# Order of maxima and values in a self-attention, PSUM banks of its last steps, and zeroing of the keys on VectorE

## The chip, the cores and the metric

The kernel runs on one core of a Trainium2 chip. The metric is the device time in microseconds of one execution, and a kernel's figure is the median of its runs. A profile is one execution of its own, taken by the hardware profiler.

## What is computed

Four stages are applied to x (4 samples, 1024 tokens, 256 channels), all in float32. L0 is a routed mixture of three small networks and a gate. L1 and L2 are transformer blocks, each with self-attention, cross-attention over 77 context tokens and a feed-forward part; L3 is one more cross-attention. The self-attentions matter here; this is the one of L1, cut:

```python
def mha(x, ctx, wq, bq, wk, bk, wv, bv, wo, bo, mask=None):   # 16 heads of 16 channels
    q = (x @ wq + bq).reshape(Bq, Nq, H, HD)
    k = (ctx @ wk + bk).reshape(Bq, Nk, H, HD)
    v = (ctx @ wv + bv).reshape(Bq, Nk, H, HD)
    scores = jnp.einsum('bqhd,bkhd->bhqk', q, k) / np.sqrt(HD)
    attn = jax.nn.softmax(scores, axis=-1)
    return jnp.einsum('bhqk,bkhd->bqhd', attn, v).reshape(Bq, Nq, D) @ wo + bo
h = layernorm(x, ln1_g, ln1_b)
h = mha(h, h, sa_wq, sa_bq, sa_wk, sa_bk, sa_wv, sa_bv, sa_wo, sa_bo)
x = x + h + t_sa[:, None, :]
```

L2 has the same with a modulated layernorm and with `x = x + g_sa * x_sa`.

## The kernel before

**The order of work.** One loop over the four samples does L0. A second one ("blocks") does L1, L2 and L3 for one sample per pass. Its work is a list of named steps, PASS, written by `pass_schedule`: L1sa, L1ca, L1mlp, L2sa, L2ca, L2mlp, L3ca. Every engine walks through the same list and issues its own part of each step; semaphore counts are taken from the position of a step in the list. So the list is the order on each of the in-order engines. SP's DMAs have a list of their own (`stack_maxima`, the DMA is L591).

**The steps of a self-attention.** Almost all matmuls go through a helper at L634, so its line stands for most of TensorE's rows.

- N, T: a half of the tokens is normalised (DVE L1417) and transposed (TensorE L919, copied by ACT L1149).
- P, K: a projection of q or k (c = half of the channels, n = half of the tokens), split into a high and a low part by ACT and POOL; then selection matmuls that place pairs of heads into qs or ks, one head in each 64-row stack. K carries a pattern of four letters, one for each tile: "a" and "d" say that ACT or DVE evicts it, "-" that it isn't done in this step; small letters are matmuls over 32 rows, capital letters matmuls over all 128 rows.
- V: the values of two token tiles (8 matmuls), evicted by ACT (L1325). V0 to V3 make up all eight tiles.
- A(g, n, t, j): scores of one token tile against all keys, only for their maxima: two matmuls into two neighbouring banks and a DVE tensor_reduce over 1024 elements into mxh (L1683). A group (g, n), four heads and half of the tokens, has 16.
- both, M: DVE joins the maxima of a group into mx (L1692); TensorE transposes mx (L1036, four transposes), ACT copies the result to mrow (L1350), SP's DMA puts mrow into row 32 of the qs stacks. The pair is called the group's turn. With that row the scores come out with the maximum taken off.
- S(g, n, kt, j): transposed scores of one key tile (kt, 8 of them) and one head; ACT's exp writes probs (L1366). PV multiplies probs by v into bank 7.
- O, OT: behind the last key tile of a group ACT copies bank 7 to ow (L1372), TensorE transposes ow (L1082), DVE divides by the sums (L1708, L1710) into tok.
- aT, o: tok is transposed (L1091, ACT L1377) and multiplied by the output weights; DVE adds to x (L1649; in L2 after the gate, L1644). scond, R and add put bias rows onto x (ACT L1299, TensorE, DVE L1601, POOL L1787).

A self-attention is 8 groups of 8 units, unit u being (g, n, kt). The order in a unit is: S for two heads, OT if one is due, PV of the unit two before, S for two more heads, and then as many maxima as `more` allows. The maxima run ahead of the scores: before unit 0 stands the front with 19 of them, the first 16 each with a projection, stack or values step beside it. Units 0 to 4 then take 2, 3, 3, 3, 3 maxima, the later ones 2 each, and the last falls in unit 52. The turn of a group stands inside the maxima of the next: "both" follows two of them and M follows three (for the very first turn, "both" follows none and M one).

**Banks.** In a self-attention TensorE's steps other than PV take banks from banks 0 to 6 by least recent use (`shared`); A takes two neighbours. A step waits until the engine that read the bank before is done. The other modules have small rings of their own: 0 and 1 (with 6 and 7 for maxima) and 2 to 5.

**The cross-attention behind a self-attention** begins inside its tail (`cross_lead`). Its keys are placed in kz, which POOL has to zero first ("zero", L1803). In `cross_attention` the stack of q ("AAAA", ACT L1334) stands ahead of the transpose of the second token half, T(1).

## Time and profile before

| | us |
|---|---|
| median of 3 runs | 4191.32 (4186.39 to 4198.61) |
| profiled execution | 4198.08 |
| its span, first to last instruction | 4196.3 |
| TensorE busy | 3678.6 (88%) |
| ACT busy | 2353.3 (56%) |
| DVE busy | 2214.9 (53%) |
| granted TensorE clock, mean | 0.933 |

Busy shares are averages over stages with different limits. The granted clock is a share of full speed: 1.00 is 2.4 GHz, 0.50 is 1.2 GHz. In a row of the timeline, `[0.51 <-DVE mxh L1683]` says that the engine sat idle for 0.51 us and that the DVE instruction of line 1683, writing mxh, ended this. PE is TensorE, PEld its loading of weights. x2 behind an operation is two instructions in a row, and the time is that of both together. In the table by stretch, x behind a busy time is the number of instructions.

### The profile page before, as it was taken

To read this page: it belongs to the slowest core of one execution; us is meant where nothing else is said; L and a number is where in the kernel's file an instruction comes from. 1 tells how busy PE (TensorE), PEld (TensorE's weight loads), DVE (VectorE), ACT (ScalarE), POOL (GpSimd) and SP (SyncE) were. 2 spreads that over 40 slices of the span, in tenths; PEclk is the share of its full clock that TensorE was granted. 3 is DMA by queue.
4 is the path that set the end of the run, shared out by engine and by line. 5 is a ranking of instruction groups with operands and counts; after the bars stand their busy time and mean duration, and the time that the engine had idled before them with its cause. 6 is when DMAs were issued, how large, how long until landed. Compare 5 with 4: busy or idle time off the path is not lost.

```text
span 4196.3 us, 65738 instructions
## 1 busy us (share of the span) xinstructions
PE 3678.6 (88%) x20057; PEld 2127.3 (51%) x20057; DVE 2214.9 (53%) x3552; ACT 2353.3 (56%) x4082; POOL 864.1 (21%) x558
## 2 busy tenths in 40 slices
PE   7999988889888878889888788898889788898888
PEld 5777674346434743356336543464347333563356
DVE  4332435743674447644755457436744566437644
ACT  2333335764676456764666457646764567546754
POOL 3222221014102410033005110241023100240041
PEclk8999998999999989999999989999999899999999
DMA  3000110001000010000000100010000100000010
GB/s 125 31 1 31 31 37 34 2 27 41 1 1 12 31 42 1 16 32 21 1 1 33 50 1 1 27 41 1 1 12 31 42 1 17 31 21 1 1 31 22
DMA packets 70782, 92.76 MB, mean 22 GB/s; under 512 B 9227, under 2 KB 57934, under 8 KB 70350
## 3 DMA queue, kind: packets, MB, share of 16 engines
q1 hardware_dynamic: 40958, 63.40, 4.5%
q10 hardware_dynamic: 29520, 25.39, 1.9%
q8 instruction: 181, 2.97, 0.3%
q14 instruction: 123, 1.01, 0.1%
HBM read 77.96 MB, written 9.50 MB: 21 GB/s over the span
## 4 chain that ended last, share of the span: by engine, by line
issue 79%; POOL 16%; PE 3%; DVE 0%; POOLq 0%; ACT 0%; DMA 0%; SPq 0%; ACTq 0%; DVEq 0%
POOL hidl L1761 3%; PE ps L634 3%; POOL hidl L1796 3%; POOL x L1787 2%; POOL ql L1820 2%; POOL small L1721 1%; POOL kl L1820 1%; POOL hTl L1728 1%; POOL W2h L1811 1%; POOL W1h L1811 1%; POOL W1l L1813 0%; POOL W2l L1813 0%; POOL kz L1803 0%; DMA sel_in<-in_sel 0%; DVE tok L1417 0%
## 5 line engine op out<-in xcount | busy, mean ns | idle before, releaser
L1683 DVE TENSOR_REDUCE mxh<-ps 128x2 f32<-128x1024 f32 x1024 | 1211.1, 1220 | 419.9 <-PE ps L634 416.2
L1366 ACT ACTIVATE probs<-ps 128x512 f32<-128x512 f32 (+1 forms) x2176 | 1215.0, 629 | 380.2 <-PE ps L634 374.5
L634 PE MATMUL ps<-probs,v 128*32 128x512 f32 (+1 forms) x4864 | 680.0, 632 | 3.8 <-ACT probs L1366 3.8
L634 PE MATMUL ps<-qs,ks 64*128 64x512 f32 x2048 | 559.4, 486 | 11.0 <-DVE mxh L1683 9.7
L634 PEld LDWEIGHTS ps<-qs,ks 64*128 64x128 f32 x2048 | 261.4, 190 | 539.6 <-ACT probs L1366 355.1
L1721 POOL TENSOR_TENSOR small<-small 128x4 f32<-128x4 f32 x66 | 68.3, 1035 | 2246.6 <-DVE small L1411 2246.6
L634 PE MATMUL ps<-ks,qs 64*128 64x512 f32 x2048 | 413.0, 462 | 128.2 <-DVE mxh L1683 100.3
L634 PEld LDWEIGHTS ps<-ks,qs 64*128 64x128 f32 x2048 | 202.7, 191 | 331.5 <-DVE mxh L1683 226.8
L634 PE MATMUL ps<-hT,slot 128*128 128x512 f32 x448 | 247.7, 687 | 24.2 <-ACT hT L1149 9.2
L634 PE MATMUL ps<-slot,hT 128*128 128x256 f32 x896 | 238.6, 415 | 14.8 <-ACT hT L1377 9.3
L1680 DVE TENSOR_REDUCE mx<-ps 128x4 f32<-128x312 f32 x384 | 167.4, 478 | 117.6 <-PE ps L634 113.9
L1334 ACT ACTIVATE qs<-ps,cols 128x512 fp32r<-128x512 f32 x288 | 178.6, 692 | 73.7 <-PE ps L634 73.7
L634 PEld LDWEIGHTS ps<-slot,hT 128*128 128x128 f32 x896 | 177.7, 207 | 75.3 <-issue 21.7
L1761 POOL TENSOR_TENSOR hidl<-hid,hidh 128x512 fp32r<-128x512 f32 x96 | 127.6, 1333 | 334.6 <-ACT hid L1233 334.6
L634 PEld LDWEIGHTS ps<-probs,v 128*32 128x32 f32 (+1 forms) x4864 | 97.0, 109 | 157.9 <-issue 78.2
L1820 POOL TENSOR_TENSOR ql<-whole,qh 128x512 fp32r<-128x512 f32 x80 | 102.0, 1275 | 316.1 <-ACT whole L1319 316.1
L1796 POOL TENSOR_TENSOR hidl<-hid,hidh 128x512 fp32r<-128x512 f32 x128 | 161.9, 1291 | 10.9 <-ACT hid L1384 9.0
L1649 DVE TENSOR_TENSOR x<-x,ps 128x512 f32<-128x512 f32 x80 | 55.0, 687 | 189.9 <-PE ps L634 189.9
L1230 ACT ACTIVATE hidh<-ps,cols 128x512 fp32r<-128x512 f32 x96 | 66.3, 690 | 158.2 <-PE ps L634 158.1
L1708 DVE RECIPROCAL rc<-ps 128x16 f32<-128x16 f32 x160 | 40.6, 254 | 203.0 <-PE ps L1082 203.0
L634 PE MATMUL ps<-kz,qs 128*128 128x156 f32 x768 | 131.2, 296 | 17.9 <-ACT hT L1149 5.7
L634 PE MATMUL ps<-W2h,hidh 128*128 128x256 f32 x512 | 145.2, 284 | 0.0
(220 smaller groups left out, 6134.1 us busy)
## 6 DMA issues: line engine op xcount, KB each, us to landing
slot<-in_L_w SPq DMA_DIRECT2D x8, 1024.0 KB, 7.7
slot<-in_L_fc_w SPq DMA_DIRECT2D x8, 1024.0 KB, 5.2
adw<-in_L_adaln_w SPq DMA_DIRECT2D x4, 1536.0 KB, 6.5
xin<-in_x ACTq DMA_DIRECT2D x5, 1024.0 KB, 5.6
x_after_block<-x ACTq DMA_DIRECT2D x20, 256.0 KB, 2.3
xin<-x_after_block ACTq DMA_DIRECT2D x5, 1024.0 KB, 5.5
ew<-in_L_e_w SPq DMA_DIRECT2D x6, 768.0 KB, 12.3
x<-in_x ACTq DMA_DIRECT2D x4, 1024.0 KB, 7.3
```

The costliest lines, as they stand in the source:

```text
L634: return pe.matmul(out, lhsT, rhs, start=start, stop=stop)
L1230: act.activation(hidh0[:, (E * n + e) % 2, m % 4, :], src, ACT.Silu, bias=col("L0_e_b1", m))
L1334: ins = act.activation(qs[:, pair, n * HALF:(n + 1) * HALF], ps[:, b, :], ACT.Identity, bias=qs_rows)
L1366: ins = act.activation(dst, src, ACT.Exp, scale=SCALE)
L1680: dve.tensor_reduce(mx[:, z, t, j0:j0 + GH], ps[:, a, 0:GH * SP_].rearrange("p (j s) -> p j s", s=SP_), AX.X, ALU.max, negate=True).then_i ...
L1683: dve.tensor_reduce(mxh[:, z, t, j // 2, j % 2, :], ps[:, a:a + 2, :], AX.X, ALU.max, negate=True).then_inc(dve_done, M.add(dve_done, name))
L1721: pool.tensor_tensor(rstd[:, tt], ve[:, tt], nhalf[:, tt], ALU.pow).then_inc(pool_done, M.add(pool_done, (tag, "rstd", h)))
L1761: pool.tensor_tensor(hidl0[:, (E * n + e) % 2, m % 4, :], hid0[:, m % 4, :], hidh0[:, (E * n + e) % 2, m % 4, :].bitcast(F32), ALU.subtrac ...
L1787: pool.tensor_tensor(x[:], xin[:] if tag == "L1sa" else x[:], rrow[:].unsqueeze(1).to_broadcast([P, NT, D]), ALU.add).then_inc(pool_done, ...
L1796: pool.tensor_tensor(hidl[:, n, m, :], hid[:, n, m, :], hidh[:, n, m, :].bitcast(F32), ALU.subtract).then_inc(pool_done, M.add(pool_done, ...
L1811: pool.tensor_tensor(hi[:], w, zero.unsqueeze(2).to_broadcast(w.shape), ALU.add).then_inc(pool_done, M.add(pool_done, name + ("hi",)))
L1820: pool.tensor_tensor(lo[:, c, part], whole[:, whole_of(name)[0], 0:kn], hi[:, c, part].bitcast(F32), ALU.subtract).then_inc(pool_done, M.a ...
```

## The change

- Turns: "both" comes directly behind the last maximum of its group, and M four maxima of the next group later (one later for the very first turn).
- Values: V1 and V2 leave the front, V3 leaves unit 1, and they stand in units 0, 1 and 2, between the first two scores and PV.
- Front: the stacks of q(1,0), q(1,1) and k(1,1) are done in capitals, over 128 rows (k(1,1) was already); the four half stacks of q have an empty place after each; both half stacks of k(1,1) move from unit 0 to ahead of it. The front holds 20 maxima instead of 19, units 0 to 3 take 3 each and the others 2, and the last is in unit 51.
- End of a self-attention: aT(0), o0, o1 and the next N0 come one unit earlier. OT(3,1), aT(1,0), aT(1,1), o2 and o3 use the banks 6, 7, 6, 7, 6 and are no longer in the shared order.
- Cross-attention behind a self-attention: "zero" is a DVE memset behind T(0) and OT(3,1) instead of a POOL addition ahead of T(0); T(1) and eight maxima come before the q stack "AAAA", which had stood behind four.

```diff
@@ -148,17 +148,16 @@
             for n in range(NH):
                 scores = [("A", g, n, t, j) for t in range(TPH) for j in range(GH)]
 
-                first = 0 if (g, n) <= (0, 1) else 2
-                maxima += scores[:first] + turn[:1] + scores[first:first + 1] + turn[1:] + scores[first + 1:]
+                behind = 1 if (g, n) == (0, 1) else 4
+                maxima += turn[:1] + scores[:behind] + turn[1:] + scores[behind:]
                 turn = [("both", g, n), ("M", g, n)]
         maxima += turn
 
-        def halves(which, c, n):
-            return [("K", "aa--", which, c, n), ("K", "--aa", which, c, n)]
-
-        beside = ([("P", "k", 1, 0)] + halves("q", 0, 1) + [("P", "q", 1, 1)] + halves("k", 1, 0) + [("P", "k", 1, 1)] + halves("q", 1, 0)
-                  + [("V", 1)] + halves("q", 1, 1))
-        later = [("K", "AA--", "k", 1, 1), ("K", "--AA", "k", 1, 1), ("V", 3)]
+        def halves(which, c, n, who="a"):
+            return [("K", 2 * who + "--", which, c, n), ("K", "--" + 2 * who, which, c, n)]
+
+        beside = ([("P", "k", 1, 0)] + halves("q", 0, 1) + [("P", "q", 1, 1)] + halves("k", 1, 0) + [("P", "k", 1, 1)]
+                  + [w for k in halves("q", 1, 0, "A") + halves("q", 1, 1, "A") for w in (k, None)] + halves("k", 1, 1, "A"))
         taken = 0
 
         def more(upto):
@@ -171,13 +170,10 @@
         first_slot = GH * TPH
         for i in range(first_slot):
             more(i + 1)
-            put(tag, *beside[i:i + 1])
-        assert len(beside) <= first_slot
+            put(tag, *[w for w in beside[i:i + 1] if w])
         more(first_slot + 1)
-        put(tag, *[("scond",)] * (tag == "L1sa"), ("R",), ("add",))
-        more(first_slot + 2)
-        put(tag, ("V", 2))
-        lead = first_slot + 3
+        put(tag, *beside[first_slot:], *[("scond",)] * (tag == "L1sa"), ("R",), ("add",))
+        lead = first_slot + 4
         more(lead)
         lag = 2
         units = [(g, n, kt) for g in range(GROUPS) for n in range(NH) for kt in range(NT)]
@@ -186,6 +182,8 @@
         for u in range(end + lag):
             if u < end:
                 put(tag, *[("S",) + units[u] + (j,) for j in range(2)])
+            if u < 3:
+                put(tag, ("V", u + 1))
             if turn is not None:
                 put(tag, ("OT",) + turn)
                 turn = None
@@ -197,23 +195,22 @@
                     turn = unit[:2]
             if u < end:
                 put(tag, *[("S",) + units[u] + (j,) for j in range(2, GH)])
-                put(tag, *(later[:2] if u == 0 else later[2:] if u == 1 else []))
-                more(lead + min(3 * u, 2 * u + 4) + 2)
-
-            if u == end - 5:
+                more(lead + min(3 * (u + 1), 2 * (u + 1) + 4))
+
+            if u == end - 6:
                 put(tag, *[("aT", 0, c) for c in range(KC)])
-            elif u in (end - 4, end - 3):
-                put(tag, ("o", u - end + 4))
-            elif u == end - 2:
+            elif u in (end - 5, end - 4):
+                put(tag, ("o", u - end + 5))
+            elif u == end - 3:
                 put(follow, ("N", 0))
 
     def cross_lead(tag, before):
 
         first, then = projections("q", 0)
         if before:
-            put(tag, ("zero",), ("T", 0))
+            put(tag, ("T", 0))
             put(before, ("OT", GROUPS - 1, NH - 1))
-            put(tag, *projections("k", 0))
+            put(tag, ("zero",), *projections("k", 0))
             put(before, *[("aT", NH - 1, c) for c in range(KC)])
             put(tag, ("K", "dddd", "k", 0, 0), first)
             put(before, ("o", 2))
@@ -229,11 +226,10 @@
         def singles(which, c, n):
             return [("K", "-" * i + "A" + "-" * (PAIRS // KC - 1 - i), which, c, n) for i in range(PAIRS // KC)]
 
-        put(tag, *maxima[:4], ("K", "AAAA", "q", 1, 0))
         if before:
-            put(tag, ("T", 1), *maxima[4:8], ("P", "q", 0, 1), *maxima[8:10], ("V", 0), ("P", "q", 1, 1))
+            put(tag, *maxima[:4], ("T", 1), *maxima[4:8], ("K", "AAAA", "q", 1, 0), ("P", "q", 0, 1), *maxima[8:10], ("V", 0), ("P", "q", 1, 1))
         else:
-            put(tag, *maxima[4:6], ("P", "q", 1, 1), *maxima[6:10], ("V", 0))
+            put(tag, *maxima[:4], ("K", "AAAA", "q", 1, 0), *maxima[4:6], ("P", "q", 1, 1), *maxima[6:10], ("V", 0))
         put(tag, *maxima[10:14], ("K", "aaaa", "q", 0, 1), *maxima[14:16])
         put(tag, ("add",), ("M", 0, 0))
         for i, k in enumerate(singles("q", 1, 1)):
@@ -860,6 +856,7 @@
                 "L2mlp": [("L2mlp_g", silu_of(adw[:, :, 5 * D:6 * D]) + [pick("g_ff")]), ("L2mlp", [pick("fc2_b")])],
                 "L3ca": [("L3ca", [pick("bp")])],
             }
+            TAIL = {("OT", (GROUPS - 1, NH - 1)): 0, ("aT", (NH - 1, 0)): 1, ("aT", (NH - 1, 1)): 0, ("o", (2,)): 1, ("o", (3,)): 0}
             rings = {"small": 0, "single": 0, "wide": 0}
             used = [0] * 7
             M.open("blocks")
@@ -887,6 +884,9 @@
                         return tuple(range(b, b + count))
 
                     def small():
+                        if not alone and (kind, step[1:]) in TAIL:
+                            b = 6 + TAIL[kind, step[1:]] % 2
+                            return b, (b,)
                         if not alone:
                             banks = shared(2 if kind == "A" else 1)
                             return banks[0], banks
@@ -1334,7 +1334,7 @@
                                 ins = act.activation(qs[:, pair, n * HALF:(n + 1) * HALF], ps[:, b, :], ACT.Identity, bias=qs_rows)
                             elif cross:
                                 if tag != "L3ca":
-                                    act.wait_ge(pool_done, upto(pool_done, (tag, "zero")))
+                                    act.wait_ge(dve_done, upto(dve_done, (tag, "zero")))
                                 for e in range(2):
                                     r = stacked(e, 0, STACK)
                                     ins = act.activation(kz[r, pair, e, :], ps[r, b, 0:SP_], ACT.Identity, bias=ks_rows[r])
@@ -1604,6 +1604,9 @@
                             dve.wait_ge(conditions_loaded, upto(conditions_loaded, "all"))
                             dve.tensor_scalar(mrowb[:], mi[:], 0.0, MASKED, ALU.is_equal, ALU.mult).then_inc(dve_done, M.add(dve_done, "mrowb"))
                             dve.tensor_scalar(mcolb[:], mic[:], 0.0, MASKED, ALU.is_equal, ALU.mult).then_inc(dve_done, M.add(dve_done, "mcolb"))
+                    elif kind == "zero":
+
+                        dve.memset(kz[:].bitcast(F32), 0.0).then_inc(dve_done, M.add(dve_done, name))
                     elif kind == "mod" and tag == "L2sa":
                         dve.wait_ge(mm_done, upto(mm_done, name))
                         b = M.where(name)
@@ -1662,7 +1665,7 @@
                             b = M.where((tag,) + stack)
                             if cross:
                                 if tag != "L3ca":
-                                    dve.wait_ge(pool_done, upto(pool_done, (tag, "zero")))
+                                    dve.wait_ge(dve_done, upto(dve_done, (tag, "zero")))
                                 for e in range(2):
                                     r = stacked(e, 0, STACK)
                                     ins = dve.tensor_scalar(kz[r, pair, e, :], ps[r, b, 0:SP_], ks_rows[r], None, ALU.add)
@@ -1795,12 +1798,6 @@
                         pool.wait_ge(act_done, upto(act_done, name))
                         pool.tensor_tensor(hidl[:, n, m, :], hid[:, n, m, :], hidh[:, n, m, :].bitcast(F32), ALU.subtract
                                            ).then_inc(pool_done, M.add(pool_done, name))
-                    elif kind == "zero":
-
-                        before = MODULES[[m for m, _ in MODULES].index(tag) - 1][0]
-                        pool.wait_ge(mm_done, upto(mm_done, (before, "S", GROUPS - 1, NH - 1, NT - 1, GH - 1)))
-                        flat = kz[:].rearrange("p c e s -> p (c e s)")
-                        pool.tensor_tensor(flat, zero.to_broadcast(flat.shape), zero.to_broadcast(flat.shape), ALU.add).then_inc(pool_done, M.add(pool_done, name))
                     elif kind == "split":
 
                         w, hi, lo, loaded = (W1, W1h, W1l, slot_loaded[2]) if step[1] == "W1" else (W2, W2h, W2l, slot_loaded[3])
```

## Rows read from the trace of the kernel before

**Rows 1.** The page: busy time of each engine, share, instructions.

```profile
PE 3678.6 (88%) x20057; PEld 2127.3 (51%) x20057; DVE 2214.9 (53%) x3552; ACT 2353.3 (56%) x4082; POOL 864.1 (21%) x558
```

**Rows 2.** Timeline, steady unit: start, busy us, engine, line, operation.

```profile
739.85 0.73 PE L634 MATMUL ps<-ks,qs 64*128 64x512 f32 x4 [0.51 <-DVE mxh L1683]
...
740.39 2.36 DVE L1683 TENSOR_REDUCE mxh<-ps 128x2 f32<-128x1024 f32 x2 [0.59 <-PE ps L634]
```

**Rows 3.** Stretches: start:end, length, busy PE, PEld, DVE, ACT, POOL, clock, DMA.

```profile
654.50:692.60 38.10, 32.16 (x114) 15.88 (x115) 23.30 (x23) 17.74 (x29) 8.35 (x4) 0.82 0.00 1
692.60:726.10 33.50, 28.80 (x137) 12.74 (x136) 21.57 (x20) 20.60 (x39) 0.00 (x0) 0.90 0.00 1
726.10:854.70 128.60, 113.24 (x685) 46.79 (x688) 97.60 (x96) 90.93 (x172) 0.00 (x0) 0.96 0.01 2
...
752.40:777.20 24.80, 21.91 (x141) 9.09 (x144) 19.52 (x20) 18.15 (x36) 0.00 (x0) 1.00 0.00 1
...
1948.60:1983.40 34.80, 31.64 (x114) 15.69 (x115) 23.56 (x22) 16.25 (x27) 8.38 (x4) 0.85 0.00 1
1983.40:2015.90 32.50, 27.14 (x137) 11.58 (x136) 21.61 (x20) 20.60 (x39) 0.00 (x0) 0.95 0.00 1
2015.90:2142.50 126.60, 111.35 (x683) 46.58 (x682) 97.52 (x96) 90.56 (x172) 0.00 (x0) 0.97 0.01 1
```

**Rows 4.** Timeline, a turn of maxima and what follows.

```profile
744.71 0.68 PE L1036 MATMUL ps<-ident,mx 128*4 128x128 f32 x4 [1.17 <-DVE mx L1692]
...
745.50 0.59 ACT L1350 ACTIVATE mrow<-ps 4x512 f32<-4x512 f32 x1 [2.00 <-PE ps L1036]
...
748.95 2.36 DVE L1683 TENSOR_REDUCE mxh<-ps 128x2 f32<-128x1024 f32 x2 [3.16 <-PE ps L634]
```

**Rows 5.** Stretches of slow clock, in the front and at the turn.

```profile
676.80:690.50 13.70, 9.46 (x24) 5.50 (x22) 4.92 (x8) 2.07 (x3) 3.76 (x1) 0.50 0.00 1
745.10:748.50 3.40, 3.40 (x16) 0.99 (x15) 0.69 (x1) 1.67 (x3) 0.00 (x0) 0.50 0.01 2
```

**Rows 6.** Timeline, a unit with the transposes of ow.

```profile
758.21 0.66 PE L1082 MATMUL ps<-ident,ow 128*128 128x128 f32 x4
...
760.75 2.35 DVE L1683 TENSOR_REDUCE mxh<-ps 128x2 f32<-128x1024 f32 x2
```

**Rows 7.** Timeline behind an L2 self-attention: values, k selection.

```profile
1313.29 1.99 PE L634 MATMUL ps<-slot,hT 128*128 128x256 f32 x8 [1.36 <-ACT whole L1319]
...
1316.79 0.30 PE L634 MATMUL ps<-kh,sel 32*128 32x78 f32 x1 [1.27 <-DVE x L1649]
```

**Rows 8.** Timeline, front of the first L1 self-attention.

```profile
671.49 7.09 DVE L1683 TENSOR_REDUCE mxh<-ps 128x2 f32<-128x1024 f32 x6 [1.13 <-PE ps L634]
...
682.13 2.07 PE L634 MATMUL ps<-slot,scond 128*128 128x256 f32 x4 [2.27 <-ACT scond L1299]
...
686.85 3.77 PE L634 MATMUL ps<-slot,hT 128*128 128x256 f32 x8
```

**Rows 9.** Timeline, ACT in units without maxima.

```profile
874.03 8.03 ACT L1366 ACTIVATE probs<-ps 128x512 f32<-128x512 f32 x16 [1.47 <-PE ps L634]
```

**Rows 10.** Timeline, lead and first maxima of the L1 cross-attention.

```profile
906.48 0.90 PE L634 MATMUL ps<-kh,sel 32*128 32x78 f32 x4 [0.92 <-ACT hT L1377]
...
907.66 2.54 DVE L1668 TENSOR_SCALAR kz<-ps,cols 64x78 fp32r<-64x78 f32 x8 [3.90 <-PE ps L634]
...
924.88 2.42 ACT L1334 ACTIVATE qs<-ps,cols 128x512 fp32r<-128x512 f32 x4 [3.26 <-PE ps L634]
...
928.02 0.45 PE L634 MATMUL ps<-kz,qs 128*128 128x156 f32 x2 [1.21 <-ACT hT L1149]
```

**Rows 11.** One line: count, ns min/median/max, starts, form.

```profile
L1569 DVE MEMSET v<- x1: 3472/3472/3472, 625.4 to 625.4; 128x4096 f32 x1
```

**Rows 12.** Timeline, a cross-attention: mrow and what its DMA released.

```profile
949.70 0.57 ACT L1350 ACTIVATE mrow<-ps 16x512 f32<-16x512 f32 x1
...
953.37 0.46 PE L634 MATMUL ps<-qs,kz 64*77 64x512 f32 x2 [0.21 <-DMA qs<-mrow]
```

## The prediction

> **What bounds the kernel now.** The page comes first: TensorE is busy for 88% of the span and no other engine for more than 56% [rows 1], so the first guess is TensorE. The chain of waits on the page names nothing for most of the span, so the timeline of one steady unit of a self-attention comes next [rows 2]. There DVE reduces two maxima in 2.36 us and then waits 0.59 us for the matmuls of the next two, while TensorE itself had to wait 0.51 us for DVE before it could write them. The two form a loop through the PSUM banks: reduce, bank free, matmul, reduce. Its period is 2.36 + 0.59 = 2.95 us, 23.6 us for the 8 units of a group. What a self-attention costs beyond that is what the change can touch.
>
> The table by stage [rows 3] shows how much it is. Groups 1 to 5 of the first L1 self-attention take 128.6 us where 5 x 23.6 = 118.0 would do: 10.6 too long. Those of a later L2 one (second block) take 126.6: 8.6 too long. Group 0 takes 33.5 and 32.5 us. The front, from the first maximum to the first exponential, takes 38.1 and 34.8 us, with DVE busy for only 23.3 and 23.6 of them.
>
> Where the 10.6 us go is seen at a turn [rows 4]. TensorE arrives at the transposes of the maxima and waits 1.17 us for DVE's "both". The matmuls queued behind the transposes come late, and DVE's next reduce starts after 3.16 us of idleness where 0.59 is normal. Behind this turn there is a second loss: for 3.4 us the granted clock reads 0.50, that is 1.2 GHz [rows 5]; TensorE had stood still just before. One group in which the clock stays at 1.00 takes 24.8 us. If two of the five are like it, the other three take (128.6 - 49.6) / 3 = 26.3. So a turn costs 1.2 us by its wait (24.8 - 23.6) and a dip another 1.5.
>
> **Part 1: the turn.** "both" now stands straight behind the group's last maximum and the transposes four maxima further on. Two maxima are one unit, so "both" is by then at least one period old: the 1.17 us wait is gone, and with it what made DVE idle. The transposes remain, 0.68 us of TensorE [rows 4]; their cover is TensorE's own wait for DVE in each unit. The nearest row for work of this kind is the four transposes of ow, 0.66 us: the reduce behind them starts with no idleness at all [rows 6]. The ACT copy to mrow and the SP DMA move with the transposes; since more maxima are ahead, TensorE comes to them in the same unit as before, and nothing behind them on ACT or SP comes later. The upper end is all of the 10.6 (L1) and 8.6 us (L2). At the lower end the dips stay, three and two at 1.5 us: 6.1 and 5.6. I take 85% of the upper ends, 9.0 and 7.3, because the row of ow is the nearest; the rest is TensorE work that spills over. What is late next is the bank loop itself.
>
> **Part 2: group 0.** Its 8 units hold 20 maxima. From rows 2, a unit with three of them takes 3 x 1.18 + 0.59 = 4.1 us, so four such and four of 2.95 make 28.3 us. V1, V2, V3 (8 matmuls each, 1.99 us at full clock [rows 7]) now come in units 0, 1 and 2, between two scores and probs x v. Three maxima are six matmuls, some 1.1 us by the 0.73 us of four [rows 2], and four scores as much, so 1.99 us more fit into the 4.1 of units 0 and 1, which have no probs x v. In unit 2 probs x v adds about 1.1, and 1.0 is lost. ACT's copy of V, 0.6 us, stands beside four exponentials of 2.0 us [rows 9] and fits everywhere. The upper end is 33.5 - 29.3 = 4.2 for L1 and 3.2 for L2. At the lower end V runs at half clock (3.77 us [rows 8]) in all three units, which takes the gain and 3 us more: -3. I take 3.3 and 2.3, nearer to the upper end, since these units ran at 0.90 and 0.95 [rows 3].
>
> **Part 3: the front.** V1 leaves (DVE's wait behind it was 1.13 us), and V2, 3.77 us in which DVE soon stood idle [rows 8]: 4.9 us. Added are one more maximum and, behind the last slot, the second half stack of k11 with two ACT evictions: 0.8 us for its two matmuls at half clock (four take 0.73 at full clock, [rows 2]) and 2 x 0.6 for the evictions (four take 2.42, [rows 10]), 2.0 in sum. Net 2.9, the lower end. At the upper end the clock comes back in the 13.7 us at 0.50 [rows 5]: the four scond matmuls take 2.07 us there [rows 8] and the four rows matmuls are of the same shape, so 2.07 of both would return, and most of the 2.0 hides: 6.3 in L1; L2 has no scond, 4.9. The full-row selections (capitals) stream the same 512 columns; without a row of their own here I bound them by 0 and by 0.5 us for each of the four half stacks that are new in them, about half of what four 32-row selections take (0.90, [rows 10]), 2 us in sum, hidden by DVE's reduces in the slots where nothing now stands beside the maximum; I take nothing. I take 4.0 and 3.3 for the part, near the lower ends, because the first turn keeps only one maximum between "both" and its transposes, so the standstill before the slow stretch remains.
>
> **Part 4: the end of the maxima.** One more maximum ahead means that the last falls in unit 51. Four units without maxima take 8.03 us by ACT [rows 9], 2.0 each against 2.95: half of the difference, 0.5 us.
>
> **Part 5: tail, banks, cross lead.** OT(3,1), aT, o2 and o3 get banks 6 and 7 of their own; aT(0), o0, o1 and N0 start a unit earlier. In L1 the k selections wait 0.92 us for ACT, and the cross-attention's maxima wait 1.21 us for T(1)'s copy, which stood behind a whole q stack on ACT [rows 10]; T(0) comes perhaps 0.5 sooner, a quarter of a 2.0 us unit. Upper end 2.6, lower end 0; I take 1.5. In L2 TensorE waits 1.36 and 1.27 us at banks that ACT and DVE still read [rows 7]; with 1.2 and 0.5 as in L1 the upper end is 4.3, the lower 0; I take 3.2, as both waits are named.
>
> **Part 6: zero.** POOL's addition goes, DVE gets a memset of 1248 elements a row. The one memset in the trace does 4096 in 3.47 us [rows 11], so 1.06 us, at a place where DVE sits idle for 3.90 us before the k stack [rows 10]: nothing. Without that cover it would be 1.06 x 8 = 8.5 us in all.
>
> **The sum.** L1: 9.0 + 3.3 + 4.0 + 0.5 + 1.5 = 18.3. L2: 7.3 + 2.3 + 3.3 + 0.5 + 3.2 = 16.6. Each of the four blocks has one of both: 4 x 34.9 = 140 us. The profiled execution took 4198.1 us (1.8 more than its span), so it would take 4058; the median before is 4191.3, so 4051. All upper ends: 4 x (24.2 + 21.5) = 183, 4008. All lower ends: 4 x (6.5 + 6.0) = 50, 4141.
>
> **The rivals.** (a) The clock stays restless: 0.68 us of transposes in a full unit are followed by a stretch at half clock even without the wait. For it: the stretch of rows 5 begins within the transposes. Against: the transposes of ow are as long and fall into a group that runs at 1.00 [rows 3, 6]. Price: 5.5 dips per block at 1.5 us and 1 us at each front, 4 x 10 = 40: 4091. The Trainium skill's TensorE: Matmul & The Clock Gate, Part 4: PE-mode transpose, says that transposes do not count as busy time for the clock as matmuls do; by that rule this case would come. The group with the transposes of ow at 1.00 speaks against it at this size.
>
> (b) TensorE bounds group 0, V being paid at half clock. For it: the stretch just ahead reads 0.50 [rows 5]. Against: V has left that stretch. Price: part 2 at its lower end, 6.3 and 5.3 less, 46 in four blocks: 4097. The Trainium skill's TensorEngine Tiling (Array Packing), Key Properties, says that a change of tiling mode drains TensorE, and V between scores (64 rows) and probs x v (32 columns) adds one. By that rule each V would cost more than its 1.99 us. Nothing before shows V there; the full-size transposes between the same two cost DVE nothing [rows 6].
>
> (c) The wait only moves to the next bank, and parts 1 and 2 fall out. For it: DVE releases "both" and the banks alike. Against: the loop keeps 2.95 us in every unit but the turn's. What remains is 4 x (6.0 + 7.0) = 52: 4139.
>
> (d) It becomes slower. The first scores of a group need the row of maxima that SP's DMA puts into qs, two units (5.9 us) behind the transposes. The copy to mrow ends 1.4 us after these start [rows 4], which leaves 4.5; a landing takes 953.37 - 950.27 = 3.1 us [rows 12]; the margin is 1.4. If faster units and a busy queue eat it, TensorE stands at 7 group starts in each of 8 self-attentions, 56 in all. From 140 / 56 = 2.5 us per start the gain is gone; at 3.0 the time is 4191 - 140 + 168 = 4219. Against: a landing would have to take 7 us.
>
> **How the numbers follow.** The forecast, own range 4020 to 4075, has 0.55; more gain than that 0.04; (a) 0.17, (b) 0.12, (c) 0.06, (d) 0.03; and 0.03 that the parts lend each other's gain until nothing is measured. A measurement of this kernel tells a change from none at about 0.3%, 12.6 us. The range of 8 in 10 runs from 4015, below which only the sum of the upper ends lies, to 4105, which takes in (a) and (b). Faster: all but the last two, 0.94; same 0.03; slower 0.03.
>
> **What would show it.** Right: groups 1 to 5 near 24 us each; TensorE's transposes waiting for "both" only at the first and the last turn of a self-attention; no stretch at 0.50 behind a turn; a front of 34 us in L1 and a group 0 of 30. Wrong: transposes on time and DVE still idle for 3 us behind them (c); stretches at 0.50 elsewhere (a); V over 2 us in units 0 to 2 with DVE waiting (b); scores released by the DMA at group starts (d).

## The result, and the profile after

| | us |
|---|---|
| median of 4 runs | 4007.91 (4002.04 to 4025.84) |
| before, its 4 runs | 4194.23 (4186.39 to 4198.61) |
| ratio | 0.9565, 95% interval 0.9531 to 0.9599 |
| profiled execution, its span | 4009.09, 4007.3 |
| granted TensorE clock, mean | 0.956 (0.933 before) |

The change gives 186 us where 140 were forecast. 4008 us is below the range (4015 to 4105) and at the sum of all upper ends; the prediction gave 0.04 to more gain than its own range. The page of the changed kernel, against [rows 1]:

```profile
PE 3585.2 (89%) x20057; PEld 2109.6 (53%) x20057; DVE 2203.9 (55%) x3560; ACT 2353.9 (59%) x4082; POOL 845.4 (21%) x550
```

The instruction counts of TensorE and ACT are as before, yet TensorE is busy 93 us less: the same matmuls ran at a higher clock. The table by stretch, the answers to [rows 3], first L1 self-attention and the L2 one of the second block (front, group 0, groups 1 to 5):

```profile
654.00:685.40 31.40, 27.31 (x105) 13.28 (x103) 21.90 (x23) 19.39 (x30) 5.30 (x4) 0.96 0.01 1
685.40:718.00 32.60, 29.14 (x150) 14.56 (x149) 23.91 (x22) 19.52 (x37) 3.06 (x1) 0.93 0.01 1
718.00:836.10 118.10, 108.25 (x685) 45.89 (x688) 97.88 (x96) 90.55 (x170) 0.00 (x0) 1.00 0.01 2
1890.80:1918.70 27.90, 26.43 (x103) 12.81 (x103) 21.74 (x21) 17.90 (x28) 4.60 (x4) 1.00 0.00 1
1918.70:1949.40 30.70, 26.75 (x150) 13.31 (x149) 24.14 (x23) 19.50 (x36) 3.77 (x1) 1.00 0.00 1
1949.40:2067.40 118.00, 108.39 (x682) 46.01 (x680) 97.76 (x96) 90.43 (x171) 0.00 (x0) 1.00 0.01 2
```

Groups 1 to 5 take 118.1 and 118.0 us, which is 5 x 23.6, at a clock of 1.00. The fronts are 6.7 and 6.9 us shorter, with the clock at 0.96 and 1.00 (0.82 and 0.85 before). Group 0 is only 0.9 and 1.8 us shorter. A turn in the timeline, the answers to [rows 4]:

```profile
735.25 2.36 DVE L1686 TENSOR_REDUCE mxh<-ps 128x2 f32<-128x1024 f32 x2 [0.59 <-PE ps L630]
735.37 0.60 PE L1036 MATMUL ps<-ident,mx 128*4 128x128 f32 x4
...
738.20 2.36 DVE L1686 TENSOR_REDUCE mxh<-ps 128x2 f32<-128x1024 f32 x2 [0.60 <-PE ps L630]
```

TensorE does not wait before the transposes, and DVE is idle for 0.60 us behind them instead of 3.16. 738.20 - 735.25 is one period of 2.95 us: the transposes cost nothing.

Where the time came from, by the stages of all four blocks. Each boundary is the start of the first maximum, the start of unit 0's or a later unit's first exponential, the end of the last exponential, or the start of the cross-attention's first maximum. Means in us:

```
               front  g0    g1-5   g6,7+end  tail  rest to next self
L1 before      38.5   33.8  128.0  45.4      22.8  140.4
L1 after       32.8   32.3  118.1  46.0      19.1  139.1
L2 before      34.9   32.2  126.7  46.3      23.5  213.0
L2 after       27.9   31.2  118.2  45.8      17.6  210.3
gain, both     12.7    2.5   18.4  -0.1       9.6    4.0     = 47.1 per block, 188 in four
priced at       7.3    5.6   16.3   1.0       4.7 (both)     = 34.9 per block, 140
```

A second profile of the changed kernel has the same means within 1.4 us a stage; its tails and what follows them are in the last row of the table further below. Smaller differences between the mean lengths of two kernels are not read as effects, unless all four blocks show them alike.

### The profile page after: what moved, and what is told of

It is laid out like the page before. It is cut to its first block, busy times and chain, and to the rows that moved or that the text cites. A ratio compares the mean times of both kernels' runs of the same rounds, so it can differ in the third digit from the quotient of the medians.

```text
span 4007.3 us, 65762 instructions
## 1 busy us (share of the span) xinstructions
PE 3585.2 (89%) x20057; PEld 2109.6 (53%) x20057; DVE 2203.9 (55%) x3560; ACT 2353.9 (59%) x4082; POOL 845.4 (21%) x550
## 4 chain that ended last, share of the span: by engine, by line
issue 79%; POOL 16%; PE 3%; DVE 0%; POOLq 0%; ACT 0%; DMA 0%; SPq 0%; ACTq 0%; DVEq 0%
POOL hidl L1764 3%; POOL hidl L1799 3%; PE ps L630 3%; POOL x L1790 2%; POOL ql L1817 2%; POOL small L1724 1%; POOL kl L1817 1%; POOL hTl L1731 1%; POOL W2h L1808 1%; POOL W1h L1808 1%; POOL W1l L1810 0%; POOL W2l L1810 0%; DMA sel_in<-in_sel 0%; DVE tok L1417 0%; PE ps L1082 0%
## 5 line engine op out<-in xcount | busy, mean ns | idle before, releaser
L630 PE MATMUL ps<-probs,v 128*32 128x512 f32 (+1 forms) x4864 | 655.0, 611 | 6.3 <-ACT probs L1366 6.3
L630 PE MATMUL ps<-qs,ks 64*128 64x512 f32 x2048 | 538.3, 474 | 5.6 <-DVE mxh L1686 5.4
L630 PE MATMUL ps<-hT,slot 128*128 128x512 f32 x448 | 234.3, 654 | 27.9 <-ACT hT L1149 12.2
L630 PE MATMUL ps<-slot,hT 128*128 128x256 f32 x896 | 225.0, 398 | 9.3 <-ACT hT L1377 9.3
L630 PEld LDWEIGHTS ps<-slot,hT 128*128 128x128 f32 x896 | 168.5, 196 | 60.6 <-issue 21.6
L630 PE MATMUL ps<-W2h,hidl 128*128 128x256 f32 x512 | 147.1, 287 | 0.0
```

The source lines that it names most:

```text
L630: return pe.matmul(out, lhsT, rhs, start=start, stop=stop)
```

## The experiments

All ratios are of a kernel's runs to those of the kernel before on the same chip. For the whole change two such series exist, 0.9565 and, on another chip, 0.9551 (0.9513 to 0.9588). Single runs of one kernel differ by up to 37 us, longer ones having a lower mean clock, and L0, which no edit touches, ends between 646 and 661 us in the profiles. A gain taken from the ratio and the same gain taken from the medians can differ by 10 us. So below about 0.003 nothing is read from a ratio, and the stage lengths carry the argument.

**The turn alone**, on the kernel before:

```diff
-                first = 0 if (g, n) <= (0, 1) else 2
-                maxima += scores[:first] + turn[:1] + scores[first:first + 1] + turn[1:] + scores[first + 1:]
+                behind = 1 if (g, n) == (0, 1) else 4
+                maxima += turn[:1] + scores[:behind] + turn[1:] + scores[behind:]
```

> The kernel before with nothing changed but the place of the turns (both behind the last maximum, M four maxima further). Theory: the wait and the slow clock behind it were all that groups 1 to 5 had over 23.6 us, so they come down to 23.6 to 23.7 us each; 10.5 us per L1 and 8.6 us per L2 self-attention, 76 us in four blocks: about 4118 us, and no stretch at 0.50 behind a turn. Rival: the clock stays up only because the new front leaves it up; then dips stay in every second group and only the waits go, 1.2 us in each of 40 groups, 48 us: about 4146 us.

Ratio 0.9812 (0.9773 to 0.9850), 79 us. Groups 1 to 5 of the first L1 self-attention in this run:

```profile
725.70:846.60 120.90, 110.11 (x682) 44.89 (x681) 98.23 (x96) 90.65 (x170) 0.00 (x0) 1.00 0.01 2
```

The dips are gone without the new front, so the rival falls. That 79 us meet the expected 76 is partly luck: groups 1 to 5 are 7.2 us (L1) and 5.7 us (L2) shorter on the mean, 52 us in four blocks, and the rest is elsewhere, 1.2 and 2.0 us in each end of the self-attentions and 2.0 us in the L2 tails (the L1 tails are 1.4 us longer), none of which the expectation counted. 24.2 instead of 23.6 us per group remain: with 19 maxima ahead, "both" comes between the two maxima of a unit and holds up the second.

**The values in the front again**, on the changed kernel:

```diff
-            if u < 3:
-                put(tag, ("V", u + 1))
+# (in words) V1 in the empty place behind q(1,1)'s first half stack, V2 behind the 18th maximum, V3 in unit 1
```

> The changed kernel with the values where they were (V1 beside a maximum, V2 ahead of unit 0, V3 in unit 1). Theory: V2 costs the front its 3.8 us at half clock and uncovers a table load of 1.3 us behind ACT's copy of it, V1 about 1; group 0 wins back 2 to 4 of the 4.0 us that V costs it now. Net 2 to 3 us per self-attention, 16 to 24 us: 4024 to 4032 us. Rival: the front was shortened by the wide selections and the shorter wait at the first turn, not by V; then the time is within 5 us of 4008, fronts of 32 to 34 us in L1.

Ratio 0.9652 (0.9605 to 0.9698).

**The q stacks over 32 rows again:**

```diff
-... for k in halves("q", 1, 0, "A") + halves("q", 1, 1, "A") for w in (k, None)]
+... for k in halves("q", 1, 0) + halves("q", 1, 1) for w in (k, None)]
```

> The changed kernel with the two q stacks of the front selected over 32 rows again. Theory of the prediction: full rows cost and save nothing, within 4 us of 4008. Rival: the wide selections are what lets DVE reduce back to back in the front (eight maxima in 9.14 us), and without them the front is 1 to 3 us longer in each of 8: 4016 to 4032 us.

Ratio 0.9611 (0.9572 to 0.9650). The fronts of the second block's L2, first with the values back, then with 32-row stacks (27.90 us at 1.00 in the changed kernel):

```profile
1895.00:1927.60 32.60, 30.51 (x122) 16.09 (x122) 23.76 (x23) 19.09 (x31) 7.52 (x4) 1.00 0.00 1
```

```profile
1898.10:1927.90 29.80, 28.69 (x103) 13.30 (x103) 21.91 (x21) 17.77 (x29) 4.63 (x4) 0.83 0.00 1
```

The two edits do different things. The wide selections raise the clock from 0.83 to 1.00, but TensorE at 0.83 still nearly keeps up with DVE, so 1.9 us come of it (none in L1: 32.9 against 32.8). All four L2 fronts are alike in this. In four blocks it is 8 us of the 19 us that the ratio shows; where the others come from is not shown. The values cost the front 4.7 us at full clock, 6.2 in L1, and give back 0.7 and 1.7 in group 0 (30.5 and 30.6 there). So V is dearer in the front than in the units by 4.3 us per self-attention, where I had expected 2 to 3, and the wide selections save a little in L2.

**Own banks taken back** from the changed kernel (`TAIL = {}`):

> The changed kernel with the last steps of a self-attention back in the shared order of banks. Theory: the banks were worth the two bank waits of L2 (2.6 us) and about 1 us in L1: 4 x 3.6 = 14 us, 4022 us. Rival: the order of the steps (one unit earlier, zero, T(1)) made the gain of the tail, and banks are worth under 1 us per self-attention: within 6 us of 4008.

Ratio 0.9584 (0.9545 to 0.9622): tails 20.6 and 18.0 us instead of 19.1 and 17.6. The 20.6 hold one tail of 22.7 at a lower clock (0.85); the other three take 19.8 at 1.00. So the banks are worth 0.8 and 0.4 us here with the clock alike. That is the rival's size; the interval of the ratio holds both answers.

**The last steps one unit later again:**

> The changed kernel with aT(0), o0, o1 and N0 one unit later again. Theory: the early N0 lets T(0) and OT start without waiting and keeps TensorE from standing still, after which the projection behind ran at half clock (3.58 us before, 1.98 after in L2); so late steps cost 1.1 by the waits and 1.6 by the clock in each tail, up to 4 x 5.4 = 22 us: 4030 us. Rival, as the prediction priced it: 0.5 us in each of eight tails, 4012 us.

Ratio 0.9585 (0.9562 to 0.9608); tails 19.4 and 17.6, no different from the changed kernel's second profile (19.5 and 18.0).

**T(1) behind the q stack again:**

> The changed kernel with T(1) behind the q stack in the cross-attentions again. Theory: the 1.21 us wait of the maxima for T(1)'s copy returns in 8 cross-attentions, 10 us: 4018 us. Rival: the waits move only, since the scores need the stack that is now late; within 4 us of 4008.

Ratio 0.9628 (0.9591 to 0.9664), the largest of the three; the stages behind the tails are 2.9 and 3.4 us longer (3.5 and 2.0 against the second profile). But group 0 of L1, which the edit does not touch, is 1.5 us longer too (33.8), so some of it is scatter.

**POOL zeroes kz again:**

> The changed kernel with POOL zeroing kz ahead of T(0) again. Theory: POOL is idle there and DVE's memset stands in its wait, so both are hidden: within 4 us of 4008. Rival: POOL's 2.27 us stand ahead of its split of k, on which the k selections wait; 0.5 to 1 us in eight places, 4012 to 4016 us.

Ratio 0.9589 (0.9566 to 0.9612); tails 19.4 and 17.6 us. Taken back singly from the changed kernel, these edits lose 0.002 to 0.006 each; only T(1)'s loss stands out from the scatter.

**V1 in the front, V2 and V3 in units:**

```diff
-            if u < 3:
+            if u in (1, 2):
```

> The changed kernel with V1 beside a maximum of the front, in the first empty place of the second q stack, and V2, V3 in units 1 and 2; unit 0 holds no V. Theory: unit 0 loses the V that cost it 2.4 us at half clock, and V1 in the front costs 1.1 us at most: 1 to 2 us less per self-attention, 8 to 16 us: 3992 to 4000 us. Rival: V in the front makes the first turn stand still longer and brings the 13.7 us at half clock back, as in the run with the values in the front: 4016 us or more.

Ratio 0.9644 (0.9614 to 0.9675), a miss: the fronts are 1.1 and 1.4 us longer as expected, but group 0 did not shorten (32.8 and 33.1).

**The tail and cross part alone on the kernel before, and all of it taken back from the changed kernel** (own banks, early last steps, memset on DVE, T(1) ahead of the q stack):

> The kernel before with only the tail and cross part of the change (own banks for the last steps, aT(0), o0, o1, N0 a unit earlier, memset on DVE, T(1) ahead of the q stack). Theory: the two stages behind a self-attention are 5.1 and 8.7 us shorter in the changed kernel because of these edits alone, so they give 4 x 13.8 = 55 us here too: ratio to before 0.987. Rival, the size of the prediction: 4.7 per block, 19 us, ratio 0.9955, the rest having come from a clock that the new self-attention leaves higher.

> The changed kernel with all of the tail and cross part taken back. Theory: 55 us are lost again, 4063 us, 0.9696 of before. Rival: 19 us, 4027 us, 0.961. If the two runs of this pair do not add up to the whole change, the parts share a gain.

Alone 0.9863 (0.9827 to 0.9900), 57 us (48 by the medians). Taken back 0.9633 (0.9594 to 0.9673) where the changed kernel beside it had 0.9551: 34 us (27 by the medians). The first number is the theory's; the second is not, and lies between the two. The parts share some 20 us: with the change's self-attention the tails are 20.3 and 19.1 us even without this part, against 22.8 and 23.5.

How they share it can be read from the step lists and the rows. In the kernel before, the shared order gives o2 of L2 the bank that the q projection has just filled, and the last matmul of the next k stack the bank of o2. So TensorE waits for ACT's copy and then for DVE's addition. These are the 1.36 and 1.27 us of [rows 7]; the third block's tail has them too, at a clock of 1.00:

```profile
3091.85 1.98 PE L634 MATMUL ps<-hT,slot 128*128 128x512 f32 x4 [0.69 <-DVE kz L1668]
3095.19 1.99 PE L634 MATMUL ps<-slot,hT 128*128 128x256 f32 x8 [1.36 <-ACT whole L1319]
3097.12 0.30 PE L634 MATMUL ps<-kh,sel 32*128 32x78 f32 x3
3098.70 0.30 PE L634 MATMUL ps<-kh,sel 32*128 32x78 f32 x1 [1.28 <-DVE x L1649]
```

In the changed kernel with the whole part taken back, the order is still the shared one, but other steps stand ahead of the tail, and by the list o2 gets bank 6, whose last reader finished long before. Neither wait is there:

```profile
2979.36 1.98 PE L630 MATMUL ps<-hT,slot 128*128 128x512 f32 x4 [0.72 <-DVE kz L1668]
2981.18 1.89 PE L630 MATMUL ps<-slot,hT 128*128 128x256 f32 x8
2983.00 0.31 PE L630 MATMUL ps<-kh,sel 32*128 32x78 f32 x4
```

The new self-attention and the own banks each remove the same two waits, so the second of them to come finds nothing left.

**One edit of that part at a time on the kernel before:**

```diff
+            TAIL = {("OT", (GROUPS - 1, NH - 1)): 0, ("aT", (NH - 1, 0)): 1, ...}   # first run: banks 6 and 7
...
-        put(tag, *maxima[:4], ("K", "AAAA", "q", 1, 0))                                             # second run
+            put(tag, *maxima[:4], ("T", 1), *maxima[4:8], ("K", "AAAA", "q", 1, 0), ...)
...
-            if u == end - 5:                                                                        # third run
+            if u == end - 6:
```

> The kernel before with only the own banks 6 and 7 for the last steps of a self-attention. Theory: the wait of 1.36 and the one of 1.27 us in L2 go, and the q projection ahead of them, 3.58 us at half clock, comes back to 2: 4.2 us per block of waits and clock in L2, 0.9 in L1; 20 us, ratio 0.995. Rival, as the prediction counted the banks: 2.6 us per block, 10 us, ratio 0.9975.

> The kernel before with only T(1) and eight maxima ahead of the q stack in the cross-attentions behind a self-attention. Theory: the whole stage is paid by the clock as well as by the wait; taking this edit back from the changed kernel cost about 26 us, so it gives 25 us here, ratio 0.994. Rival, the prediction's 1.2 us wait per cross-attention, 10 us, ratio 0.9977.

> The kernel before with only aT(0), o0, o1 and N0 one unit earlier. Theory: T(0) no longer waits for N0 and OT, k come about 1.1 to 1.5 us earlier in each of eight tails, 10 us, ratio 0.9975. Rival, the prediction's 0.5 us each, 4 us, ratio 0.999.

Ratios 0.9970 (0.9948 to 0.9991), 0.9978 (0.9957 to 0.9998) and 1.0009 (0.9991 to 1.0027): 13, 9 and -4 us, together 18, where all of them with the memset gave 57. By stages, in us:

```
                 tail L1  tail L2   rest L1  rest L2
before            22.8     23.5      140.4    213.0
banks alone       19.3     18.6      141.4    213.9
T(1) alone        22.8     22.7      138.8    212.9
early alone       22.3     24.2      140.8    213.7
all, on before    18.9     17.5      138.3    212.1
all taken back    20.3     19.1      141.4    213.2
changed           19.1     17.6      139.1    210.3
changed, again    19.5     18.0      138.5    211.7
```

So on the kernel before the banks carry nearly all of the tail: 3.5 + 4.9 = 8.4 us per block, 34 in four. Their timed gain is 13. Part of this is paid back in the same profile: the stages behind are 1.0 and 0.9 us longer, and all four L2 fronts take about 37.5 us against 34.9, at 0.82 against 0.85. Part of it is scatter: the execution profiled, 4162 us, is as short as the shortest of its ten, whose median is 4179. The 22.7 of T(1) alone in L2 is not its doing, since it stands behind the tail; the kernel before has 24.4, 24.3, 22.7 and 22.7 there. These four tell what the clock is worth. The second block's L2 tail, q projection and o2, kernel before (the row of 1.99 us that [rows 7] and the prediction call values is o2, the output product of two token tiles; it has the shape of a values step, and a V takes 1.99 us too):

```profile
2195.94 3.58 PE L634 MATMUL ps<-hT,slot 128*128 128x512 f32 x4 [0.69 <-DVE kz L1668]
...
2200.87 1.99 PE L634 MATMUL ps<-slot,hT 128*128 128x256 f32 x8 [1.36 <-ACT whole L1319]
```

with the banks alone:

```profile
2186.39 1.98 PE L634 MATMUL ps<-hT,slot 128*128 128x512 f32 x4 [0.71 <-DVE kz L1672]
2188.21 1.89 PE L634 MATMUL ps<-slot,hT 128*128 128x256 f32 x8
```

and in the changed kernel:

```profile
2119.30 1.98 PE L630 MATMUL ps<-hT,slot 128*128 128x512 f32 x4 [0.71 <-DVE kz L1671]
2121.12 1.89 PE L630 MATMUL ps<-slot,hT 128*128 128x256 f32 x8
```

The wait of 1.36 us is gone, and so are 1.6 us that I had not seen as a loss: four matmuls that take 1.98 us took 3.58, at the slow clock. The tail as a whole, before and after:

```profile
2188.00:2212.50 24.50, 18.71 (x89) 10.50 (x89) 12.08 (x34) 11.50 (x26) 4.58 (x6) 0.93 0.13 43
```

```profile
2113.30:2130.91 17.61, 15.62 (x88) 9.72 (x88) 10.62 (x30) 11.46 (x26) 3.02 (x5) 1.00 0.20 60
```

3.1 us of the 6.9 are TensorE's busy time, for the same matmuls. But only the first two blocks are like this. In the third and fourth, the same four matmuls take 1.98 us and the L2 tail runs at 1.00 in the kernel before too:

```profile
3083.90:3106.70 22.80, 17.09 (x88) 9.98 (x88) 11.97 (x34) 11.51 (x26) 4.47 (x6) 1.00 0.14 47
```

There the slow stretch stands in groups 6 and 7 instead, which take 47.0 us at 0.93, where the first two blocks have 45.6 at 0.96. So of the 5.9 us that the L2 tails gained on the mean, 5.1 came with the clock at 1.00 before and after, and 0.8 is the slow stretch (1.6 us in two of four). The L1 tails read 0.93 before in all four blocks; there the q projection takes 3.21 us and the step behind it 2.40 instead of 1.98 and 1.89, 1.7 of the 3.7 us gained.

**The last turn later**, on the changed kernel:

```diff
-        maxima += turn
+                put(tag, *([("both", GROUPS - 1, NH - 1)] * (u == end - 13) + [("M", GROUPS - 1, NH - 1)] * (u == end - 11)))
```

> The changed kernel with the last turn of a self-attention (both in unit 51, its transposes in unit 53 instead of behind the last maximum). Theory: the wait of the transposes for both, about 1.5 us, goes and TensorE does not stand still, so group 6 falls from 24.6 toward 23.6 and the slow stretch behind it goes: 1.0 to 2.5 us in each of 8, 8 to 20 us: 3990 to 4000 us. Rival: that unit is bound by ACT, which has no slack there, and nothing is gained: within 4 us of 4008.

The last turn of the changed kernel, which the change had left behind its last maximum, with ACT's next rows, and that of this run:

```profile
850.09 0.72 PE L1036 MATMUL ps<-ident,mx 128*4 128x128 f32 x4 [2.43 <-DVE mx L1695]
850.85 0.59 ACT L1350 ACTIVATE mrow<-ps 4x512 f32<-4x512 f32 x1 [3.00 <-PE ps L1036]
851.46 1.93 PE L630 MATMUL ps<-probs,v 128*32 128x512 f32 x8
854.09 9.90 ACT L1366 ACTIVATE probs<-ps 128x512 f32<-128x512 f32 x20 [1.44 <-PE ps L630]
```

```profile
856.57 0.60 PE L1035 MATMUL ps<-ident,mx 128*4 128x128 f32 x4
```

Groups 6 and 7 with the last exponentials, changed kernel and this run:

```profile
836.10:882.10 46.00, 40.23 (x251) 15.41 (x250) 17.56 (x31) 35.54 (x69) 1.02 (x1) 0.96 0.10 35
```

```profile
841.00:883.00 42.00, 39.25 (x250) 15.31 (x246) 17.50 (x31) 35.28 (x69) 1.02 (x1) 1.00 0.11 39
```

4.0 us for one wait of 2.43. ACT's exponentials set the pace there, and ACT had stood idle for 3.00 us by the wait and for 1.44 more while probs x v behind it ran at half clock (1.93 us for eight that take 1.07). By the mean stage lengths the ends are 3.7 us shorter in each of eight self-attentions, 30 us. Timed it is less: ratio 0.9510 (0.9474 to 0.9546), 3994 us, against 0.9551 and 4016 for the changed kernel beside it, so 17 to 21 us. Three of the four L1 tails read 0.92 in this run and take 20.7 instead of 19.1, which is part of the difference.

> The changed kernel itself once more, beside the other three on one chip: 0.9565 of before within its interval of 0.0034, so 3998 to 4026 us where before takes 4194. It says how far small differences to it can be read.

**That, and V1 to V3 one unit later** (units 1 to 3):

> The changed kernel with the last turn two units later and V1 to V3 in units 1 to 3 instead of 0 to 2. Theory: V1 leaves the unit that runs at half clock (2.4 us lost there), one V more meets a unit with probs x v (1.0 to 1.3 us), so about 1 us per self-attention beyond the late last turn: 0.951 - 0.002 = 0.949 of before. Rival: the clock in units 1 to 3 falls as in the run with V1 in the front, 0.953 or more.

Ratio 0.9505 (0.9487 to 0.9524), 3988 us, the lowest median measured; it cannot be told from the run with the last turn alone. Its reason is refuted: group 0 takes 34.0 and 34.3 us instead of 32.3 and 31.2, the clock in the second block's L2 one being

```profile
1898.90:1933.20 34.30, 30.81 (x153) 15.12 (x155) 24.72 (x23) 19.63 (x37) 4.02 (x1) 0.90 0.00 1
```

with V no longer in unit 0, and 1.00 with it.

## Why the prediction was right or wrong

**Part 1 was right in mechanism and a little short.** 18.4 us per block against 16.3; nothing spilled over. The transposes stand in full units and the clock stays at 1.00 for 118 us, so rival (a) is out. The rule that transposes do not count as busy time for the clock (the Trainium skill, TensorE: Matmul & The Clock Gate, Part 4) costs nothing at 0.60 us of them per turn; the dips came with the standstill before them, and went with it in the run of the turn alone.

**Part 2 was overpriced**, 2.5 us against 5.6. V was taken to fit into units 0 and 1. The timeline of group 0 of the first L1 self-attention:

```profile
686.17 3.78 PE L630 MATMUL ps<-slot,hT 128*128 128x256 f32 x8
...
690.71 3.49 DVE L1686 TENSOR_REDUCE mxh<-ps 128x2 f32<-128x1024 f32 x3 [3.06 <-PE ps L630]
...
692.41 1.99 PE L630 MATMUL ps<-slot,hT 128*128 128x256 f32 x8
...
695.11 3.49 DVE L1686 TENSOR_REDUCE mxh<-ps 128x2 f32<-128x1024 f32 x3 [0.92 <-PE ps L630]
...
700.51 3.48 DVE L1686 TENSOR_REDUCE mxh<-ps 128x2 f32<-128x1024 f32 x3 [1.91 <-PE ps L630]
```

DVE waits 3.06, 0.92 and 1.91 us behind the three V where 0.6 is normal: 2.5 + 0.3 + 1.3 = 4.1, and 28.3 + 4.1 = 32.4 of the measured 32.6. Units 1 and 2 are within 0.3 us of what I summed; unit 0 is the half clock of rival (b), which thus held for one V of three in L1. In the L2 self-attention of the second block all three V take 1.99 us and the waits are 0.92, 0.92 and 1.91, 1.9 us in sum: 30.2 of the measured 30.7. So the three V cost group 0 about 2 us at full clock, of which I had 1.0, and 2.1 us more where the first of them runs at half clock. The rule that a change of tiling mode drains TensorE (the Trainium skill, TensorEngine Tiling (Array Packing), Key Properties) shows no price here: V takes 1.99 us between scores, as it does elsewhere [rows 7].

**Part 3 was mis-sized**, 12.7 us against 7.3. I took the slow stretch before the first scores for given, because the first turn would stand still as before. It does not. The first turn of the kernel before:

```profile
678.85 1.01 PE L1036 MATMUL ps<-ident,mx 128*4 128x128 f32 x4 [1.98 <-DVE mx L1692]
```

In the changed kernel the wait is 0.40:

```profile
677.00 0.60 PE L1036 MATMUL ps<-ident,mx 128*4 128x128 f32 x4 [0.40 <-DVE mx L1695]
...
681.13 1.28 ACT L1366 ACT_TABLE_LOAD   x1
681.17 1.13 PE L630 MATMUL ps<-slot,scond 128*128 128x256 f32 x4 [2.64 <-ACT scond L1299]
```

The scond matmuls take 1.13 us instead of 2.07 [rows 8], although TensorE waits longer before them. And ACT loads the table for the exponential while TensorE works. Before, ACT's copy of V2 stood ahead of it, and its 1.28 us lay open between the first scores and the first exponential:

```profile
690.66 0.60 ACT L1325 ACTIVATE v<-ps 128x512 f32<-128x512 f32 x1 [8.66 <-PE ps L634]
...
691.28 1.28 ACT L1366 ACT_TABLE_LOAD   x1
...
692.58 0.60 ACT L1366 ACTIVATE probs<-ps 128x512 f32<-128x512 f32 x1
```

That term is in neither of my ends. The run with the values back and the one with 32-row stacks divide the part: 10.9 us for V (6.2 and 4.7) and 1.9 for the wide selections, which I had entered at nothing. Together they are the 12.7 within scatter, so nothing is seen of the 2.0 us per front that I had added for the work moved into it.

**Part 4 was wrong but small:** 1.0 was priced and none came (-0.1). The last turn waited 1.53 us before; now two maxima instead of one stand in the last unit ahead of it, and it waits 2.43 us with a slow stretch behind. Moving it gave about 4 in the self-attention shown.

**Part 5 is the step that failed.** 4.7 us per block were priced, with 6.9 as the upper end; 13.6 came (tails 9.6, the stages behind them 4.0). That is 36 of the 48 us by which the sum was off. Three things were wrong in it.

- The waits were too small. In the L2 tails that ran at 1.00 before as well, 5.1 us went. 1.9 of them lie ahead of the q projection, where I had 0.5; 3.2 lie behind it, where the two named bank waits are 2.6.
- The clock had no term. Four matmuls at 3.58 instead of 1.98 us stood in plain rows. I had priced exactly this at the turn, 1.5 us a dip, and not in the tail. It is about 2.5 of the 9.6 us, so the smaller piece of the error.
- I took the part for independent of the others. The shared order of banks depends on every step ahead of the tail, so parts 1 to 4 moved the tail's banks too. With all of part 5 taken back, the tails and the stages behind them are still 5.7 us per block shorter than before (6.9 in the tails, which all run at 1.00 there, and 1.2 lost behind them). So of the 13.6 only 7.9 hang on part 5's own edits in the changed kernel, 32 us in four blocks, as timed (27 to 34). On the kernel before the same edits are worth 12.9 per block by the stages, 52 us, and 48 to 57 timed.

What stays open is why three edits that give 13, 9 and -4 us one by one give so much together. In the profiled executions, L0 left out, it is less striking: 28, 14 and -3 us, 38 in sum, against 52. The stage table says that singly they lose elsewhere part of what they win, in places at a lower clock; no run held the clock fixed, so that reading is inferred, and the memset was not run alone on the kernel before.

**Part 6** was priced at nothing; the memset takes 1.10 us (1.06 estimated), and POOL's addition put back costs 0.003 by the ratios, within their intervals. Rivals (c) and (d) did not occur: no idleness behind the transposes, and in the whole trace of the changed kernel TensorE waits for the DMA of mrow four times, 0.9 us together.

That the measured time equals the sum of the upper ends (183 us, where 186 to 188 came) is coincidence. Parts 3 and 5 went beyond their upper ends, 12.7 against 11.2 and 13.6 against 6.9, while parts 2 and 4 stayed far below theirs, 2.5 against 7.4 and -0.1 against 1.0. Only part 1, 18.4 against 19.2, is where its end says.

## What to carry to other kernels

Where a profile shows an engine waiting, look at the durations behind the wait too: at a turn the wait was 1.2 us and the dip that could follow it 1.5. And look at more than one block: the same slow stretch stood in the tail of two and ahead of it in the other two. Price every wait by the same measure, not only the one that the change is named for. Where banks are handed out by least recent use, every step moved shifts the banks of those behind it, so an edit elsewhere can remove or make a wait: print the bank and its last reader for the steps that matter, before and after. Such edits do not add up. Test the group as a whole in both directions (18 us singly, 57 together, 34 taken back), and read single ones by stage lengths.

## What the runs showed of the hardware that was not expected

With selections over all 128 rows the granted clock is 1.00 in all four L2 fronts, where the same number of matmuls over 32 rows has 0.83 in all four; TensorE's busy time is 26.4 and 28.7 us. In L1 it is 0.90 to 0.96 against 0.73 to 0.87, with no shorter front on the mean. And the clock of a stretch can change with an edit far ahead of it: the own banks, an edit in the tail alone, left all four L2 fronts, some 140 us behind the L1 tail, about 2.6 us longer than before, at 0.82 against 0.85 (0.81 in one).
